# Value products of the attention made in pairs, every fourth slot instead of one every second

## Chip, cores and metric

One core of a Trainium2 chip runs the whole kernel in one launch. The metric is the device time of the launch in microseconds: median 1300.86 of three runs (1298.59, 1300.86, 1301.11).

## What is computed

A decoder layer on x of shape (4, 512, 512), in three residual steps, each on a layer norm of what came before. For the change the middle one matters: attention of 32 query heads over 8 key heads of width 16, in which the context stands in for keys and values.

```python
x = x + mamba_mixer(layernorm(x))
# attention: B = 4 batches, KV = 8 key heads, G = 4 query heads to each, S = 512, D = 16
scores = einsum('bkgsd,bktd->bkgst', qh, kh) / sqrt(D)
weights = softmax(scores, axis=-1)
x = x + einsum('bkgst,bktd->bkgsd', weights, vh)
# feed-forward: a shared expert for all tokens and 2 of 16 routed experts for each token
x = x + shared_expert(layernorm(x)) + routed_experts(layernorm(x))
```

## The kernel before, in words

The kernel has two phases. `stream_phase` (L45 to L1194) does the mixer and the attention of all four batches, and the shared expert and router logits of the first three. `experts_phase` does the same for the last batch, then the routed experts. Between them all engines meet.

**Slots.** The order of the first phase is written out by hand: each engine runs through the same list of slots, `span = range(-LEAD, SLOTS + 8)` (L233), with LEAD = 92 and SLOTS = 4 x 64 = 256, and in each slot issues its pieces of work in a fixed order. Attention is cut into 32 groups (batch and key head), eight slots for each. `n, u = divmod(slot, UNITS)` gives the group and the slot in it. The mixer of batch b runs 92 slots ahead, so that it is over after slot 163; from then on attention is alone but for the shared expert.

**One slot on TensorE** (L1165 to L1194), in this order:

- `scores(slot)` (L1061): two bf16 matmuls of 512 columns, 128 keys against the queries of two heads, into `ps_s`. It waits for the exp of the slot before, for `ps_s` is read by it.
- transposes of queries (L932), of a finished group's output (L939, u = 3) or of its maxima (L946, u = 5), in the slots in which they fall.
- `max_scores(slot + 12)` (L1074): two bf16 matmuls into `ps_m` for the row maxima of a later group, up to slot 243. It waits for the maximum before.
- `front(a, r)` (L1105): from slot 160 on, work of the shared expert of batch a. r counts the slots from 164 + 38a. In r = 0 to 3 tokens are transposed (L1115), in r = 4 the router logits are made (L1124), then 24 matmuls of 512 columns in f32 are spread by `heavy(a, r)` (L210): for batches 0 and 1 one in three slots out of four, for batch 2 one per slot, then two. L1144 makes the gate and up products, L1157 the down product.
- `products(p)` (L1091): the value products of key tile p, four f32 matmuls of 512 columns (listed as eight), one for each query head, each in its own 32 columns of the array (`tile_position=(0, r * VW)`), summed over four key tiles in `ps_o`. It is issued in slot 2p + 3 for p = 0 to 127. It waits for the exps of slots 2p and 2p + 1.

**The other engines.** ScalarE turns `ps_s` into `prob` (L797), a ring of six slots, and waits for the product that frees a place in it (L795 and L796); it copies `ps_o` to `oT` in slot u = 2 (L840), after the fourth product of the group, which is issued in slot u = 1. VectorE takes the maximum of `ps_m` (L654), divides the output by its sum (L697, L700), and for the shared expert takes statistics and normalises (L662, L676) and does the elementwise parts (L682, L687, L692). GpSimd splits maxima and adds the output to the residual; SyncE's queue carries the loads, and the rows of maxima to `q_stack` (L296).

With `heavy`, the slot without a shared expert matmul is slot % 4 = 3 for batch 0 (slots 170 to 201) and slot % 4 = 1 for batch 1 (slots 208 to 239); products fall on all odd slots.

Of the kernel before, what the change touches and what calls it, by code (L numbers as in the profile page):

```python
# [44 lines left out]
def stream_phase(nc, dram, x1, score, ident, identb):  # L45
# [34 lines left out]
    KHALF_AT = (-32, 1)  # L80
    FRONT = SLOTS - LEAD
    WINDOW = 38
    F = 256
    E = 16
    WUP = KD * 2 * F

    with ExitStack() as ctx:
# [117 lines left out]
        def fronting(slot):  # L205

            at = slot - FRONT
            return [(a, at - WINDOW * a) for a in range(B - 1) if -4 <= at - WINDOW * a < WINDOW]

# [9 lines left out]
        def mixing(slot):  # L219

            return divmod(slot + LEAD, PERIOD)

        def batch_at(slot, at):

            b, off = divmod(slot - at, PERIOD)
            return b if off == 0 and 0 <= b < B else None
# [685 lines left out]
        def _(pe):  # L912
# [8 lines left out]
            def transpose_keys(b):  # L921
                pe.wait_ge(s_ctx, 16 * (b + 1))
                claim(s_prest, 5 * b + 1)
                for t in range(TB):
                    ins = nc.tensor.transpose(ps_t[:, t * P:(t + 1) * P], keys[:, t, :], ident[:, :])
                ins.then_inc(s_ptr, 1)

            def transpose_queries(b, c):
                pe.wait_ge(s_q, TB * (b + 1))
                claim(s_prest, 5 * b + c + 2)  # L930
                for t in range(TB):
                    ins = nc.tensor.transpose(ps_t[:, t * P:(t + 1) * P], q[:, t, c * P:(c + 1) * P], ident[:, :])  # L932
                ins.then_inc(s_ptr, 1)

            def transpose_out(n):
                pe.wait_ge(s_otc, n + 1)
                claim(s_fin, n + 1)
                for t in range(TB):
                    ins = nc.tensor.transpose(ps_t[:, t * P:(t + 1) * P], oT[:, t * P:(t + 1) * P], ident[:, :])  # L939
                ins.then_inc(s_back, 1)  # L940

            def transpose_max(n):
                pe.wait_ge(s_msplit, n + 1)
                claim(s_mev, n + 1)
                for t in range(TB):
                    ins = nc.tensor.transpose(ps_tb[:, t * P:(t + 1) * P], mpart[:, t, :], identb[:, :])  # L946
                ins.then_inc(s_mtr, 1)

            def head_means(b):
                pe.wait_ge(s_xs, KI * (b + 1))  # L950
                if b == 0:
                    pe.wait_ge(s_rest, 16 * 10)
                claim(s_gain, b + 1)
                for i in range(KI):
                    for j in range(4):
                        ins = nc.tensor.matmul(ps_t[32 * j:32 * j + 32, 0:P], head_mean[:, i, :],
                                               xz[:, i, j * P:(j + 1) * P], start=(i == 0), stop=(i == KI - 1),
                                               tile_position=(0, 32 * j))
                ins.then_inc(s_mean, 1)

            def outputs(b):
                pe.wait_ge(s_hc, NS * (b + 1))
                claim(s_yrest, b + 1)
                for k in range(NS):
                    ins = nc.tensor.matmul(ps_t[:, :], state_sum[:, k, :], csb[:, k, :],
                                           start=(k == 0), stop=(k == NS - 1))
                ins.then_inc(s_y, 1)

            def transpose_tokens(b, j):
                pe.wait_ge(s_ln, TB * b + j + 1)  # L970
                if b:
                    claim(s_xnT, TB * b + j + 1)
                turned = four[j] if b == 0 else ps_t[:, :]
                for k in range(KD):
                    ins = nc.tensor.transpose(turned[:, k * P:(k + 1) * P], xt[:, j, k * P:(k + 1) * P], ident[:, :])
                ins.then_inc(s_tr, 1)
# [72 lines left out]
            def mixer_half(b, m, h):  # L1049
                at = 2 * m + h  # L1050
                if at == 0:
                    project_steps(b)
                elif 4 <= at < 4 * GROUPS:
                    project(b, m // 2, at % 4)
                elif H2I_AT <= at < H2I_AT + KI:
                    heads_to_inner(b, at - H2I_AT)
                elif OUT_AT <= at < OUT_AT + TB * KI:
                    j, i = divmod(at - OUT_AT, KI)
                    project_out(b, j, i)

            def scores(slot):  # L1061
                n, u = divmod(slot, UNITS)
                g, t = n % G, u // 2
                if u == 0:
                    pe.wait_ge(s_mrow, 48 * (n + 1))
                if slot:
                    pe.wait_ge(s_exp, slot)
                for i in range(2):
                    r = u % 2 * 2 + i
                    ins = nc.tensor.matmul(ps_s[:, i, :], k_stack[:, g, t * P:(t + 1) * P],  # L1070
                                           q_stack[:, g * R + r, :], start=True, stop=True)
                ins.then_inc(s_sc, 1)
# [18 lines left out]
            def products(p):  # L1091
                n, t = divmod(p, TB)
                g = n % G
                pe.wait_ge(s_exp, 2 * p + 2)
                if t == 0:
                    if n:
                        pe.wait_ge(s_otc, n)
                    pe.wait_ge(s_val, n + 1)
                for r in range(R):
                    ins = nc.tensor.matmul(ps_o[r * VW:(r + 1) * VW, :], values[:, t, g, :],  # L1100
                                           prob[:, (2 * p + r // 2) % PROB, r % 2, :],
                                           start=(t == 0), stop=(t == TB - 1), tile_position=(0, r * VW))
                ins.then_inc(s_pv, 1)

            def front(a, r):  # L1105
# [25 lines left out]
                for i in heavy(a, r):  # L1131
                    if i < 16:
# [8 lines left out]
                        if i == 12:  # L1141
                            pe.wait_ge(s_fh, 2 * a + 1)
                        col = k * 2 * F + part * F + f * P
                        ins = nc.tensor.matmul(acc[part], w_shared[:, col:col + P], xnT[:, k, :],  # L1144
# [20 lines left out]
            for slot in span:  # L1165
                b, m = mixing(slot)
                n, u = divmod(slot, UNITS)
                if 0 <= slot < SLOTS:
                    scores(slot)
                if (a := batch_at(slot, K_AT)) is not None:  # L1170
                    transpose_keys(a)
                for c in range(4):
                    if (a := batch_at(slot, C_AT[c])) is not None:
                        transpose_queries(a, c)
                if u == 3 and 0 <= n - 1 < N:
                    transpose_out(n - 1)
                if u == 5 and 0 <= n + 1 < N:
                    transpose_max(n + 1)
                if b < B and m == 32:
                    head_means(b)  # L1180
                if b < B and m == 40:
                    outputs(b)
                if b + 1 < B and m in TURN_AT:
                    transpose_tokens(b + 1, TURN_AT.index(m))
                if b < B:
                    mixer_half(b, m, 0)
                if 0 <= slot + AHEAD < SLOTS:
                    max_scores(slot + AHEAD)
                if b < B:
                    mixer_half(b, m, 1)  # L1190
                for a, r in fronting(slot):
                    front(a, r)
                if slot >= 3 and slot % 2 == 1 and (slot - 3) // 2 < 2 * R * G * TB // 2:
                    products((slot - 3) // 2)  # L1194


def experts_phase(nc, dram, x1, score, ident, out):
# [9 lines left out]
    TOP = 2  # L1207
    F = 256
    KF = F // P
    TILES = (TOP * TOKENS - E) // P + E  # L1210
# [3 lines left out]
    B = 4  # L1214
    WUP = KD * 2 * F
    WCOLS = WUP + KF * D
# [7 lines left out]
    with ExitStack() as ctx:  # L1224
# [66 lines left out]
        xgT = sb("xgT", [P, 2, KD * P])  # L1291
        sg = sb("sg", [P, 2, F])
        sS = sb("sS", [P, KF, 512])
# [544 lines left out]
```

## Time and profile before

| | |
|---|---|
| median of 3 runs | 1300.86 us (1298.59 to 1301.11) |
| profiled execution, its own time | 1302.54 us |
| its span | 1300.7 us |
| TensorE matmul busy | 1224.2 us, 94% |
| VectorE busy | 684.4 us, 53% |
| ScalarE busy | 481.4 us, 37% |
| GpSimd busy | 313.6 us, 24% |
| maximum L654 | 256 times, 1224 ns each |
| exp L797 | 256 times, 1024 ns each |
| value products L1100 | 1024 listed matmuls, 605 ns each |
| mean granted TensorE clock | 0.987 |

Times are of one profiled execution. Matmuls overlap in the array, so that the duration of one listed matmul is longer than its share of the queue: the start of the next one tells that share. An idle time in brackets stands ahead of an instruction, with what ended it. "xN" is the number of listed instructions merged into a row; an f32 matmul is listed as two.

### The profile page before, as it was taken

To read this page: it belongs to the slowest core of one execution; us is meant where nothing else is said; L and a number is where in the kernel's file an instruction comes from. 1 tells how busy PE (TensorE), PEld (TensorE's weight loads), DVE (VectorE), ACT (ScalarE), POOL (GpSimd) and SP (SyncE) were. 2 spreads that over 40 slices of the span, in tenths; PEclk is the share of its full clock that TensorE was granted. 3 is DMA by queue.
4 is the path that set the end of the run, shared out by engine and by line. 5 is a ranking of instruction groups with operands and counts; after the bars stand their busy time and mean duration, and the time that the engine had idled before them with its cause. 6 is when DMAs were issued, how large, how long until landed. Compare 5 with 4: busy or idle time off the path is not lost. (4 is left out here: it accounts for less than half of the span.)

```text
span 1300.7 us, 14817 instructions
## 1 busy us (share of the span) xinstructions
PE 1224.2 (94%) x5045; PEld 508.3 (39%) x5046; DVE 684.4 (53%) x1110; ACT 481.4 (37%) x681; POOL 313.6 (24%) x459
## 2 busy tenths in 40 slices
PE   4989989999999999999999999999978999999996
PEld 2444433333333434333333333333334444444442
DVE  5843585655687465667564766767347222212211
ACT  1311223533554443555353455555510122222221
POOL 3312310221320220221022121111102244333443
PEclk9999999999999999999999999999987999999998
DMA  6320775103274201263400245000029465577641
GB/s 175 100 87 21 184 153 106 31 13 110 68 146 77 66 22 25 82 129 80 100 12 13 94 82 78 34 2 2 33 74 338 103 142 123 154 219 214 177 82 23
DMA packets 113218, 122.71 MB, mean 94 GB/s; under 512 B 19024, under 2 KB 78544, under 8 KB 112896
## 3 DMA queue, kind: packets, MB, share of 16 engines
q1 hardware_dynamic: 102624, 100.76, 29.8%
q0 software_dynamic: 10528, 21.12, 7.9%
q8 instruction: 36, 0.59, 0.2%
q14 instruction: 30, 0.25, 0.1%
HBM read 96.20 MB, written 28.97 MB: 96 GB/s over the span
## 5 line engine op out<-in xcount | busy, mean ns | idle before, releaser
L654 DVE TENSOR_REDUCE mx<-ps_m 128x2 f32<-128x1024 f32 x256 | 313.3, 1224 | 263.1 <-PE ps_m L1087 261.6
L797 ACT ACTIVATE prob<-ps_s 128x1024 f32<-128x1024 f32 x256 | 262.2, 1024 | 380.0 <-PE ps_s L1070 380.0
L1012 PE MATMUL acc<-xnT,wring 128*128 128x512 f32 x560 | 279.7, 599 | 3.5 <-DVE xz L574 1.8
L1708 PE MATMUL ps_gu<-ring,xgT 128*128 x376 | 176.9, 593 | 1.5 <-issue 1.5
L1087 PE MATMUL ps_m<-k_stack,q_stack 96*128 96x512 bf16 x512 | 153.0, 380 | 9.0 <-DVE mx L654 7.3
L1070 PE MATMUL ps_s<-q_stack,k_stack 99*128 99x512 bf16 x512 | 153.8, 382 | 4.4 <-ACT prob L797 4.1
L1442 DVE COPY xgT<-ps_x 128x512 f32<-128x512 f32 x47 | 32.5, 692 | 207.7 <-PE ps_x L1680 203.2
L1100 PE MATMUL ps_o<-prob,values 128*32 128x512 f32 x1024 | 136.4, 605 | 0.0
L1012 PEld LDWEIGHTS acc<-xnT,wring 128*128 128x128 f32 x560 | 102.6, 190 | 69.7 <-issue 34.6
L1402 POOL DMA_INDIRECT out<-y,dest x47 | 74.5, 1585 | 158.8 <-DMA out<-y,dest 115.4
L1070 PEld LDWEIGHTS ps_s<-q_stack,k_stack 99*128 99x128 bf16 x512 | 35.5, 97 | 182.4 <-issue 133.3
L1708 PEld LDWEIGHTS ps_gu<-ring,xgT 128*128 128x128 f32 x376 | 67.6, 190 | 69.8 <-issue 69.8
L1087 PEld LDWEIGHTS ps_m<-k_stack,q_stack 96*128 96x128 bf16 x512 | 45.9, 98 | 123.3 <-issue 76.5
L1724 PE MATMUL ps_yy<-ring,hT 128*128 x188 | 88.5, 593 | 0.9 <-ACT hT L1590 0.9
L1042 PE MATMUL acc<-wring,xz 128*128 128x512 f32 x168 | 85.2, 596 | 0.0
L574 DVE SCALAR_TENSOR_TENSOR xz<-acc,convw,xz 128x511 f32<-128x511 f32 (+2 forms) x84 | 62.7, 746 | 4.2 <-ACT xz L875 2.3
L1597 ACT ACTIVATE y<-ps_yy,share 128x512 f32<-128x512 f32 x47 | 32.3, 687 | 86.3 <-PE ps_yy L1724 77.4
L411 POOL TENSOR_SCALAR mneg<-mx 128x16 f32<-128x16 f32 x32 | 10.0, 313 | 190.2 <-DVE mx L654 190.2
L1389 POOL DMA_INDIRECT xg<-xn_rows,token x47 | 46.7, 993 | 23.4 <-issue 12.5
L1100 PEld LDWEIGHTS ps_o<-prob,values 128*32 128x32 f32 x1024 | 20.1, 108 | 82.1 <-issue 65.4
L1585 ACT ACTIVATE sg<-ps_gu 128x256 f32<-128x256 f32 x47 | 18.0, 384 | 83.1 <-PE ps_gu L1708 81.8
L1144 PE MATMUL acc<-xnT,wring 128*128 128x512 f32 x96 | 48.6, 594 | 0.0
(255 smaller groups left out, 1215.6 us busy)
## 6 DMA issues: line engine op xcount, KB each, us to landing
ring<-in_w_experts SPq DMA_DIRECT2D x96, 256.0 KB
wring<-in_w_in SPq DMA_DIRECT2D x80, 256.0 KB, 3.5
q_stack<-part_rows SPq DMA_DIRECT2D x96, 128.0 KB, 4.8
wring<-in_w_out SPq DMA_DIRECT2D x32, 256.0 KB, 2.7
part_rows<-part SPq DMA_DIRECT2D x20, 384.0 KB, 3.9
xt<-in_x SPq DMA_DIRECT2D x16, 256.0 KB, 4.3
k_stack<-part_rows SPq DMA_DIRECT2D x48, 64.0 KB, 4.0
xn_rows<-xt SPq DMA_DIRECT2D x3, 1024.0 KB, 4.2
```

Of the source, the lines that this page charges most:

```text
L574: ins = nc.vector.scalar_tensor_tensor(out=xz[:, i, tap:], in0=bank(b, 5 + i)[:, :SEQ - tap], scalar=convw[:, i, 3 - tap:4 - tap], in1=xz[ ...
L654: nc.vector.tensor_reduce(mx[:, n % G, 2 * u:2 * u + 2], ps_m[:, :, :], AX.X, ALU.max).then_inc(s_max, 1)
L797: nc.scalar.activation(prob[:, slot % PROB, :, :], ps_s[:, :, :], ACT.Exp, scale=SCALE).then_inc(s_exp, 1)
L1012: ins = nc.tensor.matmul(bank(b, n), weights, xnT[:, k, :], start=(k == 0), stop=(k == KD - 1))
L1042: ins = nc.tensor.matmul(bank(b, OUT_BANK + j), gated[i][:, j * P:(j + 1) * P], ring[:, w % RING, :], start=(i == 0), stop=(i == KI - 1))
L1070: ins = nc.tensor.matmul(ps_s[:, i, :], k_stack[:, g, t * P:(t + 1) * P], q_stack[:, g * R + r, :], start=True, stop=True)
L1087: ins = nc.tensor.matmul(ps_m[:, i, :], q_stack[0:KQ, g * R + r, t * P:(t + 1) * P], k_stack[0:KQ, g, :], start=True, stop=True)
L1100: ins = nc.tensor.matmul(ps_o[r * VW:(r + 1) * VW, :], values[:, t, g, :], prob[:, (2 * p + r // 2) % PROB, r % 2, :], start=(t == 0), sto ...
L1144: ins = nc.tensor.matmul(acc[part], w_shared[:, col:col + P], xnT[:, k, :], start=(k == 0), stop=(k == KD - 1))
L1402: pool.indirect_dma_start(out=out[:, :], out_offset=bass.IndirectOffsetOnAxis(ap=dest[:, n:n + 1], axis=0), in_=y[:, n % YB, :], in_offset ...
L1708: ins = nc.tensor.matmul(ps_gu[p][:, :], xgT[:, p, k * P:(k + 1) * P], weights(own)[:, k * 2 * F:(k + 1) * 2 * F], start=(k == 0), stop=(k ...
L1724: ins = nc.tensor.matmul(ps_y[p][:, :], hT[:, p, k * P:(k + 1) * P], weights(own)[:, WUP + k * D:WUP + (k + 1) * D], start=(k == 0), stop= ...
```

## The change

From slot ALONE = FRONT + 3 = 167 on, TensorE skips `products` in the slots in which p is even, and makes that product directly before the next, odd one. Up to slot 166 nothing differs. Products 82 to 127 are made in 23 pairs, in slots 169, 173 and so on to 257.

```diff
     WINDOW = 38
+    ALONE = FRONT + 3
     F = 256
...
                 for a, r in fronting(slot):
                     front(a, r)
                 if slot >= 3 and slot % 2 == 1 and (slot - 3) // 2 < 2 * R * G * TB // 2:
-                    products((slot - 3) // 2)
+                    p = (slot - 3) // 2
+                    if slot < ALONE:
+                        products(p)
+                    elif p % 2:
+                        products(p - 1)
+                        products(p)
```

## Rows read from the trace of the kernel before

**Rows 1.** Busy time by stretch: slots 170-201, 210-237, and behind the first phase

```profile
core 0: us, PE busy (x) PEld busy (x) DVE busy (x) ACT busy (x) POOL busy (x), PEclk, DMA share, GB/s
753.67:827.81 74.14, 72.22 (x353) 24.38 (x349) 51.85 (x63) 39.14 (x45) 15.37 (x37) 1.00 0.42 70
844.98:907.72 62.74, 62.59 (x303) 20.17 (x299) 41.31 (x46) 33.57 (x38) 7.20 (x24) 1.00 0.01 2
...
962.85:1020.00 57.15, 45.04 (x163) 23.33 (x164) 39.90 (x162) 6.48 (x12) 11.20 (x14) 0.79 0.78 265
```

**Rows 2.** Timeline, TensorE matmuls, slots 190 to 193: start us, duration us, line, shapes

```profile
799.33 0.60 PE L1070 MATMUL ps_s<-q_stack,k_stack 99*128 99x512 bf16 x2
799.77 0.60 PE L1087 MATMUL ps_m<-k_stack,q_stack 96*128 96x512 bf16 x2
800.20 1.02 PE L1144 MATMUL acc<-xnT,wring 128*128 128x512 f32 x2
801.06 0.59 PE L1070 MATMUL ps_s<-q_stack,k_stack 99*128 99x512 bf16 x2
801.68 0.61 PE L1087 MATMUL ps_m<-k_stack,q_stack 96*128 96x512 bf16 x2
802.22 1.06 PE L1100 MATMUL ps_o<-prob,values 128*32 128x512 f32 x8
803.22 0.61 PE L1070 MATMUL ps_s<-q_stack,k_stack 99*128 99x512 bf16 x2
803.66 0.60 PE L1087 MATMUL ps_m<-k_stack,q_stack 96*128 96x512 bf16 x2
...
804.96 0.59 PE L1070 MATMUL ps_s<-q_stack,k_stack 99*128 99x512 bf16 x2
805.58 0.60 PE L1087 MATMUL ps_m<-k_stack,q_stack 96*128 96x512 bf16 x2
806.02 1.02 PE L1157 MATMUL acc<-wring,th 128*128 128x512 f32 x2
806.97 1.06 PE L1100 MATMUL ps_o<-prob,values 128*32 128x512 f32 x8
807.97 0.39 PE L1070 MATMUL ps_s<-q_stack,k_stack 99*128 99x512 bf16 x1
```

**Rows 3.** Timeline of ScalarE and VectorE, slot 192

```profile
803.86 1.02 ACT L797 ACTIVATE prob<-ps_s 128x1024 f32<-128x1024 f32 x1 [1.14 <-PE ps_s L1070]
...
804.29 1.23 DVE L654 TENSOR_REDUCE mx<-ps_m 128x2 f32<-128x1024 f32 x1 [0.74 <-PE ps_m L1087]
```

**Rows 4.** Timeline, TensorE, scores of slots 248 and 249, without max pairs

```profile
931.21 0.60 PE L1070 MATMUL ps_s<-q_stack,k_stack 99*128 99x512 bf16 x2
...
932.93 0.60 PE L1070 MATMUL ps_s<-q_stack,k_stack 99*128 99x512 bf16 x2 [0.26 <-ACT prob L797]
```

**Rows 5.** Timeline, TensorE, matmuls in four 32-column tiles, and the next

```profile
634.58 1.95 PE L956 MATMUL ps_t<-xz,head_mean 128*32 128x128 f32 x64 [0.24 <-DVE ao L700]
636.46 1.12 PE L1012 MATMUL acc<-xnT,wring 128*128 128x512 f32 x2
...
837.99 1.08 PE L1124 MATMUL acc<-xnT,gate_w 128*32 128x128 f32 x32
839.00 0.39 PE L1070 MATMUL ps_s<-q_stack,k_stack 99*128 99x512 bf16 x1
```

**Rows 6.** Timeline, TensorE, scores that begin slots 186, 206, 210, 214 and 218

```profile
790.12 0.61 PE L1070 MATMUL ps_s<-q_stack,k_stack 99*128 99x512 bf16 x2
...
837.02 0.60 PE L1070 MATMUL ps_s<-q_stack,k_stack 99*128 99x512 bf16 x2
...
844.98 0.60 PE L1070 MATMUL ps_s<-q_stack,k_stack 99*128 99x512 bf16 x2
...
854.18 0.60 PE L1070 MATMUL ps_s<-q_stack,k_stack 99*128 99x512 bf16 x2
...
862.82 0.39 PE L1070 MATMUL ps_s<-q_stack,k_stack 99*128 99x512 bf16 x1
```

**Rows 7.** Timeline, TensorE, max pair of slot 238

```profile
908.87 0.39 PE L1087 MATMUL ps_m<-k_stack,q_stack 96*128 96x512 bf16 x1 [0.55 <-DVE mx L654]
```

## Prediction

> **What bounds the kernel now.** The change touches TensorE's order only from slot 167 on, where the mixer is over and attention runs beside the shared expert. I read the busy time by stretch first [rows 1]: TensorE is listed busy for 72.22 of 74.14 us in slots 170 to 201 (the first batch's shared expert) and for 62.59 of 62.74 in slots 210 to 237 (the second's), at a granted clock of 1.00, VectorE for 70 and 66%. That looks like a TensorE bound, and there every switch saved would be time saved. The page warns that ends of matmuls are modelled, so I went on to the matmuls one by one [rows 2]. They show four slots in a row, from the start of one slot's scores to the next: 1.73, 2.16, 1.74 and 3.01 us, 8.64 in sum. From start to start, the score pair takes 0.44 us of the queue, the max pair 0.44, a shared expert matmul ("F") 0.86, a product 1.00 after an entry of 0.09 to 0.10 (F to product 0.95 instead of 0.86, max to product 0.54 instead of 0.44). In the second and fourth slot the max pair starts 0.62 after the scores instead of 0.44: TensorE waited there. So there are two loops beside the queue [rows 2, 3]:
> - scores to exp 0.64, exp 1.02, exp to the next scores 0.08: at least 1.74 us per slot (ScalarE's loop). Where the max pairs are over, 0.44 + 0.86 = 1.30 us of matmuls fill a product-free slot and the next scores still start after 1.72, with 0.26 idle behind the exp [rows 4].
> - max pair to its maximum 0.63, maximum 1.23, to the next max pair 0.06: at least 1.92 us (VectorE's loop).
>
> A product-free slot has 0.44 + 0.44 + 0.86 = 1.74 of matmuls. The pair of a slot without and a slot with product is what hides both loops: while the product runs, the maximum and the exp catch up. That is the cover the change takes away.
>
> **The change, step by step.** It moves 23 products (82, 84 to 126) two slots later, each beside the next one, in slots 169, 173 to 257. Nothing is added: no instruction, DMA or semaphore. No wait gets later in effect: product p waits for exps that the scores before it in the queue have waited for already; the probability buffer of slot s + 1 needs the first product of the burst of slot s, and its exp stands behind scores that come after that burst anyway; the fourth product of a group stays in its slot, so the copy of the output, its transpose and POOL's add keep theirs. SP and POOL are passed by nothing.
>
> *The burst itself.* The trace has no product right behind another. Bounds: at most as alone, 0.09 + 1.00 = 1.09 us; at least 0.86, what F shows for the same 512 columns in f32 [rows 2]. The nearest rows are matmuls in the same four 32-column tiles back to back [rows 5]: 16 of 128 columns take 1.01 to the next instruction, 32 take 1.88, so 16 more cost 0.87, or 0.87 for four tiles of 512 columns. I take 0.86: entry and exit (0.23) are paid once per burst. A pair then costs 0.09 + 0.86 + 1.00 = 1.95. The Trainium skill, "TensorEngine Tiling (Array Packing)", Key Properties, says that changing the tiling mode drains the array; by that rule alone each burst saves one drain and the change is a gain, which is the first rival below. The trace agrees that a switch costs something: the 0.09 ahead of a product and the 0.14 behind it, beyond 0.86, show it.
>
> *First batch's shared expert, slots 170 to 201.* Its matmul-free slot is every fourth, slot % 4 = 3, and the bursts fall on slot % 4 = 1, which has an F. So four slots become F; nothing; F; F + two products. From the end of a burst, t = 0:
> - Slot 2: scores 0, max 0.44, F 0.88; next scores 1.74. Its maximum runs 1.07 to 2.30.
> - Slot 3: max pair at 2.36, queue empty at 2.80. Exp 2.38 to 3.40, next scores 3.48: the queue idles 0.68. Maximum 2.99 to 4.22.
> - Slot 0: max pair only at 4.28, F at 4.72, next scores 5.58. Maximum 4.91 to 6.14.
> - Slot 1: max pair 6.20, F 6.64 to 7.50, two products to 9.45.
>
> 9.45 against 8.64 is +0.81. With the transposes of outputs (0.52 in slot 3) and maxima (0.40 in slot 1) four slots take 9.21 now [rows 2, 6]; by the same steps they become 1.74 + 1.74 + 2.44 + 4.09 = 10.01, +0.80: what the transpose adds in slot 3 is absorbed, but it delays the maximum and comes back in slot 0. Eight such groups of four: **+6.4**.
>
> *Second batch's, slots 210 to 237.* The slots without F are now the burst slots, so work is spread evenly: F 1.74; F 1.92 (max loop); F 1.92; burst 0.62 + 0.44 + 1.95 = 3.01: 8.59, against 8.64 now; with transposes 9.15 against 9.20 [rows 6]. Seven groups: **-0.4**.
>
> *Between.* Slots 206 to 209 (router logits, one F) take 7.96 now [rows 6]; three slots then go by the loops, 1.96 + 1.74 + 1.92, and the burst takes 3.01: **+0.7**. Slots 202 to 205, by the same steps: +0.1. In 238 to 241 the third batch's statistics already hold the max pairs up [rows 7]; one product leaves the waiting and one comes back two slots later: 0. Slots 242 to 245: -0.2. Slots 246 to 253 (F each, no max pairs): 3 x 1.72 + 0.44 + 0.86 + 1.95 = 8.41 against 8.22, twice, less carry: +0.2. The end, slots 254 to 263, is a full queue in which the saved switch counts: -0.3.
>
> Sum: 6.4 - 0.4 + 0.7 + 0.1 - 0.2 + 0.2 - 0.3 = **+6.5 us**. The profiled execution took 1302.54 (span 1300.7 and 1.8 around it), 1.7 over the median 1300.86; against its own time the sum gives 1309.0, against the median **1307.4**. The expert phase behind comes as a block, later by the same amount. What could make it a little more: in slots 174 and 185 and the like a tanh or a multiplication of F stands between the exps or maxima, uncovered now (a few tenths).
>
> **Rivals.**
> 1. *Faster: the queue is the bound.* If TensorE worked through these slots without waiting, as the 62.59 of 62.74 us in [rows 1] suggest, 23 bursts save 0.23 each: -5.3, 1295.6. It decides if the product-free slots last as long as their matmuls; a slot with neither F nor product would then last 0.88. Against it: the max pair 0.62 instead of 0.44 behind the scores [rows 2], and 1.72 us for 1.30 us of matmuls [rows 4]. The point of no change is a second product costing 0.57 (6.5/23 = 0.28 less than I take), below the 0.86 of its columns. 6%.
> 2. *Nothing is saved in the burst.* The second product costs 1.09 because it waits for the first in the same bank. Then 23 x 0.23 = 5.3 more: +11.8, 1312.7. For it: no row shows it at 512 columns. Against: [rows 5]. 13%.
> 3. *No measurable change.* The loops lose 6.5, but slots go faster than my chain has it, or the clock, granted at 0.79 on the mean over the 57 us behind the hand-over to the expert phase [rows 1], comes back a few us earlier. 1301. 8%.
> 4. *It doesn't do what it says*: the condition takes every odd product from 83 to 127 with its forerunner, no product is lost or made twice, so nothing here; under 1%, inside 3.
>
> **How the numbers follow.** The forecast, slower by 4 to 9, has 73%. The range starts at 1303.6 (+2.7: half of the first batch's loss gone) and ends at 1312.6 (rival 2); outside are rivals 1 and 3 and what overshoots 2. A measurement of this kernel tells about 0.2% (2.6 us) from no change. Faster by more 6%; within 8%; slower 86%.
>
> **What would show it.** Slots 170 to 201 about 6.4 us longer (74.1 to 80.5), slots 210 to 237 shorter by 0.4 (62.7 to 62.3); three out of four slots at 1.74 to 2.44; a new idle time of TensorE of 0.6 to 0.7 us behind the exp in slots % 4 = 3 up to 199; the second product 0.86 behind the first; exp and maximum unchanged in number and duration. Wrong would be: the second product at 1.09 (rival 2); first stretch unchanged (rival 1: my loops are not loops); a loss that is spread evenly over both batches, which would mean that the place of the free slot doesn't matter.

## The result, and the profile after

The changed kernel takes 1307.09 us (median of 7 runs, 1303.43 to 1314.69), the kernel before 1300.34 (7 runs, 1296.87 to 1301.11). The ratio is 1.0055, with a 95% interval of 1.0031 to 1.008: slower by 0.3 to 0.8%. Forecast were 1307.4 and slower. Three executions took far longer than the others of their kernel (2495.8 us of the kernel before, 1597.72 us with bursts from slot 205 alone, 4680.28 us of the kernel before with the free slot moved), and the ratios leave them out.

The profiled execution of the changed kernel is the longest of the seven (1314.69 us, span 1312.9). Read as a whole, it would put the loss at 12 us. It has to be read by stretch. Slot 164, three slots ahead of the first difference, begins at 740.46 instead of 738.51 us: 2.0 us of scatter in code that is the same. From there to the first instruction of the expert phase the changed kernel takes 233.67 us instead of 225.88, which is **+7.8**. The expert phase, the same code again, takes 338.8 instead of 336.3.

Busy time by stretch, of the kernel after, for the two stretches of [rows 1] (slots 170 to 201, slots 210 to 237):

```profile
core 0: us, PE busy (x) PEld busy (x) DVE busy (x) ACT busy (x) POOL busy (x), PEclk, DMA share, GB/s
755.69:836.95 81.26, 74.23 (x353) 26.08 (x349) 52.81 (x64) 39.11 (x45) 14.49 (x36) 0.98 0.37 64
854.98:917.72 62.74, 62.07 (x302) 21.72 (x299) 41.73 (x45) 33.43 (x38) 7.18 (x24) 1.00 0.01 2
```

Nearly all of the loss is in the first batch's stretch: 74.14 became 81.26 us, +7.1. The second batch's, with seven bursts in it, took 62.74 before and takes 62.74 now. The matmuls listed are as many as before (353, 302 against 303); TensorE now has 7 us there without any, 5 more than before.

The timeline of TensorE's matmuls for slots 190 to 193, which answers to [rows 2]:

```profile
805.46 0.61 PE L1071 MATMUL ps_s<-q_stack,k_stack 99*128 99x512 bf16 x2
805.90 0.60 PE L1088 MATMUL ps_m<-k_stack,q_stack 96*128 96x512 bf16 x2
806.33 1.02 PE L1145 MATMUL acc<-xnT,wring 128*128 128x512 f32 x2
807.19 0.60 PE L1071 MATMUL ps_s<-q_stack,k_stack 99*128 99x512 bf16 x2
807.82 0.61 PE L1088 MATMUL ps_m<-k_stack,q_stack 96*128 96x512 bf16 x2
808.99 0.59 PE L1071 MATMUL ps_s<-q_stack,k_stack 99*128 99x512 bf16 x2 [0.57 <-ACT prob L798]
809.74 0.60 PE L1088 MATMUL ps_m<-k_stack,q_stack 96*128 96x512 bf16 x2 [0.15 <-DVE mx L655]
810.18 1.02 PE L1158 MATMUL acc<-wring,th 128*128 128x512 f32 x2
811.04 0.59 PE L1071 MATMUL ps_s<-q_stack,k_stack 99*128 99x512 bf16 x2
811.66 0.60 PE L1088 MATMUL ps_m<-k_stack,q_stack 96*128 96x512 bf16 x2
812.11 1.02 PE L1158 MATMUL acc<-wring,th 128*128 128x512 f32 x2
813.06 1.92 PE L1101 MATMUL ps_o<-prob,values 128*32 128x512 f32 x16
814.92 0.39 PE L1071 MATMUL ps_s<-q_stack,k_stack 99*128 99x512 bf16 x1
```

The four slots last 1.73, 1.80, 2.05 and 3.88, together 9.46 us (805.46 to 814.92), where they took 8.64. Read the second slot first: its matmuls need 0.88 us of the queue, and it lasts 1.80, of which 0.57 are put down to the exp. Then the max pair of the third slot comes 0.75 behind its scores instead of 0.44, for the maximum. The burst is the row of 16 listed matmuls: 1.86 us from its start to the next scores, after an entry of 0.09. One product alone has 1.00 in [rows 2]; so the second adds 0.86.

### The profile page after: what moved, and what is told of

The parts are those of the page before. It is cut to its first block and busy times, and to the rows that moved or that the text cites. A ratio compares the mean times of both kernels' runs of the same rounds, so it can differ in the third digit from the quotient of the medians.

```text
span 1312.9 us, 14813 instructions
## 1 busy us (share of the span) xinstructions
PE 1222.5 (93%) x5041; PEld 512.7 (39%) x5046; DVE 684.4 (52%) x1110; ACT 480.7 (37%) x681; POOL 313.0 (24%) x459
## 5 line engine op out<-in xcount | busy, mean ns | idle before, releaser
L1101 PE MATMUL ps_o<-prob,values 128*32 128x512 f32 x1024 | 131.6, 602 | 0.0
```

## The experiments

All kernels are judged by the length of the two stretches (slots 170 to 201 and 210 to 237) in their profile, where a slot repeats within a few hundredths, and by the time only where that can tell. Each ratio is to runs of the kernel before that were made beside it.

**Is it where the free slot stands?** The changed kernel, with the free slot of batch 0 moved onto the burst slots:

```diff
             if a < 2:
-                return () if s % 4 == 1 else (3 * (s // 4) + (s % 4 + 1) // 2,)
+                return () if s % 4 == (3, 1)[a] else (3 * (s // 4) + (s % 4 if a == 0 else (s % 4 + 1) // 2),)
```

> The changed kernel, with batch 0's free slot (no shared expert matmul) moved from slot % 4 = 3 to slot % 4 = 1, onto its burst slots, as batch 1 has it. Theory (the burst costs what it leaves uncovered, and only where a slot with neither matmul nor product arises): slots 170 to 201 fall from 81.3 us to about 74 (the kernel before: 74.1), four plain slots there to 8.6, and the time lands within 0.1% of the kernel before, about 1301. Rival (two products in a row delay scores and maxima, wherever they stand): slots 170 to 201 stay near 81, and the time at 1307.

Measured: 1299.41 us (12 runs), ratio 0.9987 (0.9963 to 1.0012). The stretches, in the order of above:

```profile
754.32:828.49 74.17, 71.53 (x352) 26.09 (x349) 51.36 (x62) 39.01 (x45) 14.51 (x36) 1.00 0.39 70
846.52:909.27 62.75, 62.08 (x303) 21.73 (x299) 41.72 (x45) 33.44 (x38) 7.17 (x24) 1.00 0.01 2
```

All 23 bursts are still there, and 7.1 us are gone by moving eight empty places two slots on. Of these, 0.48 are a fall of the granted clock in the profiled execution of the changed kernel, told of in the last section; 6.6 are the place (80.79 us for the same bursts at full clock, below). A burst as such costs nothing that can be seen in these stretches.

The opposite edit, `(1, 3)[a]` with the forms of the two batches exchanged, takes batch 1's free slot off its bursts:

> The changed kernel, with batch 1's free slot moved from slot % 4 = 1 to slot % 4 = 3, away from its burst slots, as batch 0 has it. Theory: slots 210 to 237 grow from 62.7 us by 7 x 0.8 = 5.6 to 68.4, the whole by about 6 over the changed kernel, 12.7 over the kernel before: 1313. Rival (the loss belongs to batch 0, through the query transposes or the statistics in its slots): slots 210 to 237 stay at 62.7, the time at 1307.

Measured: 1313.62 us (8 runs), ratio 1.0095 (1.0061 to 1.013).

```profile
751.97:833.15 81.18, 74.15 (x353) 26.09 (x349) 52.79 (x64) 39.12 (x45) 14.50 (x36) 0.98 0.37 64
852.04:920.80 68.76, 63.23 (x302) 21.22 (x298) 42.58 (x47) 33.43 (x38) 7.18 (x24) 1.00 0.01 2
```

The second stretch grew by 6.0, the first kept its loss. So the loss doesn't belong to batch 0 (query transposes, statistics); the same pattern costs about the same in the other batch, 0.86 us per group of four against 0.83.

**Which bursts cost?** Bursts up to slot 202 alone, and from 205 alone:

```diff
-                    if slot < ALONE:
+                    if slot < ALONE or slot > 202:
```

> The changed kernel with bursts in slots 169 to 201 alone, single products from 203 on. Theory: the whole loss is here, +6.6 to +7.3 over the kernel before, 1307. Rival (each burst costs about the same 0.3 us): 9 of 23 bursts, +2.6, 1303.

```diff
-    ALONE = FRONT + 3
+    ALONE = FRONT + 39
```

> The changed kernel with single products up to slot 202 and bursts in slots 205 to 257 alone. Theory: +0.7, 1301; slots 210 to 237 unchanged at 62.7. Rival (each burst costs the same 0.3 us): 14 of 23 bursts, +4.1, 1304.5.

Measured: 1305.79 us (10 runs), ratio 1.0039 (1.0015 to 1.0063), for the first; 1301.22 us (12 runs), ratio 0.9993 (0.9965 to 1.0022), for the second. First the two stretches of the one, then of the other:

```profile
751.16:831.95 80.79, 72.72 (x352) 25.52 (x348) 52.46 (x64) 39.12 (x45) 14.50 (x36) 1.00 0.37 65
849.12:911.86 62.74, 62.59 (x303) 20.17 (x299) 41.29 (x46) 33.55 (x38) 7.16 (x24) 1.00 0.01 2
```

```profile
757.70:831.82 74.12, 72.21 (x352) 24.37 (x349) 51.82 (x63) 39.15 (x45) 15.36 (x37) 1.00 0.40 70
849.85:912.59 62.74, 62.07 (x302) 21.74 (x299) 41.73 (x45) 33.46 (x38) 7.20 (x24) 1.00 0.01 2
```

The nine bursts of the first (the one in slot 169 and eight in the stretch) carry +6.65 in slots 170 to 201. Its time alone (0.15 to 0.63% longer) would leave the rival's 1303 open; the stretch doesn't. The fourteen of the second carry +0.9 up to slot 253, of which 0.7 are in slots 206 to 209, and with the end +0.6 from slot 164 to the hand-over. A price per burst is excluded.

**Is the place of the free slot worth something by itself?** The kernel before with the same edit of `heavy` as in the first experiment:

> The kernel before with batch 0's free slot moved from slot % 4 = 3 to slot % 4 = 1, without bursts. Theory: with one product in every odd slot it doesn't matter which of the odd slots has the shared expert matmul; slots 170 to 201 stay at 74.1 us and the time at that of the kernel before. Rival (the new place of the free slot is itself worth some 7 us and would have hidden the burst's loss in the aligned kernel): slots 170 to 201 at 67, the time at 1294.

Measured: 1297.95 us (10 runs), ratio 0.9985 (0.9964 to 1.0007); first stretch:

```profile
756.73:829.98 73.25, 72.11 (x353) 24.43 (x349) 50.92 (x63) 39.01 (x45) 15.31 (x37) 1.00 0.42 71
```

The first seven groups of four slots last as long as before, within 0.04 us. The 0.9 us less come from the eighth, slots 198 to 201 (9.75 instead of 10.60), in which VectorE also takes the statistics of batch 1, and half of that returns in slots 202 to 205 (9.67 instead of 9.21). So the rival's 7 us aren't there, and the place alone is worth 0.4. Against this control, the fair one for the aligned kernel, the bursts aren't quite free: the aligned kernel takes 1.1 us more from slot 164 to the expert phase, with +0.9 in slots 198 to 201, +0.7 in 206 to 209 and -0.3 each in 202 to 205 and at the end, but less than 0.1 in the first seven groups together.

**Two loops, or one?** The maxima over half the keys, in the kernel before and in the changed one. The other half of the maximum is left out; the subtracted value is a little lower for some rows, the rest is computed as before.

```diff
-                nc.vector.tensor_reduce(mx[:, n % G, 2 * u:2 * u + 2], ps_m[:, :, :], AX.X, ALU.max).then_inc(s_max, 1)
+                nc.vector.tensor_reduce(mx[:, n % G, 2 * u:2 * u + 2], ps_m[:, :, 0:SEQ // 2], AX.X, ALU.max).then_inc(s_max, 1)
```

> The kernel before with the row maxima taken over the first 256 of 512 keys (that part of the maximum is left out; the sums are otherwise the same). The maximum should take about 0.7 us instead of 1.23 and VectorE's loop 1.4 instead of 1.92, under ScalarE's 1.74. Expected: four plain slots of batch 0 from 8.64 to 8.28, slots 170 to 201 to 72.5, slots 210 to 237 to 61.6. It is the reference for the next run.

> The changed kernel with the maxima over half the keys. Theory (two loops share the loss): with VectorE's loop short, ScalarE's alone is left: four plain slots of batch 0 are 1.74 + 1.74 + 1.74 + 3.69 = 8.91, slots 170 to 201 about 75.6, that is +3.1 over the kernel before with half maxima where the changed kernel lost 7.1; slots 210 to 237 turn into a gain of 1.5 (60.1). Rival (VectorE's loop is all of it): 170 to 201 no longer than in the other. Rival (neither loop, the products' own length): the loss stays at 7.

Measured in one run each: 1279.28 and 1282.14 us; a maximum took 0.69 us. Stretches of the first kernel, then of the second:

```profile
738.61:810.74 72.13, 71.46 (x353) 24.96 (x349) 35.27 (x62) 39.15 (x45) 14.91 (x37) 1.00 0.43 72
827.71:889.27 61.56, 61.56 (x303) 20.95 (x299) 27.32 (x45) 33.57 (x38) 7.20 (x24) 1.00 0.01 2
```

```profile
737.16:812.71 75.55, 71.54 (x353) 25.73 (x349) 36.13 (x64) 39.11 (x45) 14.38 (x35) 1.00 0.39 69
830.07:890.14 60.07, 60.07 (x303) 21.96 (x299) 28.08 (x47) 33.45 (x38) 7.16 (x24) 1.00 0.01 2
```

With VectorE's loop short, the bursts cost 3.4 us in the first stretch instead of 6.65, and win 1.5 in the second instead of nothing. Both loops are in it, with about half each. VectorE's half is shown by the edit; no run has a shorter exp, so ScalarE's is what remains, read from the trace. What is left of ScalarE's is seen in the timeline of the second kernel, slots 191 and 192:

```profile
785.82 0.60 PE L1071 MATMUL ps_s<-q_stack,k_stack 99*128 99x512 bf16 x2
786.26 0.60 PE L1088 MATMUL ps_m<-k_stack,q_stack 96*128 96x512 bf16 x2
787.62 0.59 PE L1071 MATMUL ps_s<-q_stack,k_stack 99*128 99x512 bf16 x2 [0.77 <-ACT prob L798]
788.05 0.59 PE L1088 MATMUL ps_m<-k_stack,q_stack 96*128 96x512 bf16 x2
```

The free slot still lasts 1.80 us for 0.88 of matmuls, all for the exp; the max pair behind it is no longer late (0.43 after the scores).

**What does a pair save?** The front's work of a burst slot put between the two products:

```diff
+                apart = slot >= ALONE and slot % 4 == 1 and (slot - 3) // 2 < 2 * R * G * TB // 2
+                if apart:
+                    products((slot - 3) // 2 - 1)
                 for a, r in fronting(slot):
                     front(a, r)
...
                     elif p % 2:
-                        products(p - 1)
                         products(p)
```

> The changed kernel with the shared expert's work of a burst slot put between the two products instead of ahead of both, so that each product is entered and left on its own. Theory (a pair saves one switch of 0.23 us): +0.23 in each of the some 15 burst slots that hold such work, slots 170 to 201 from 81.3 to 83.1, the time +3.4 over the changed kernel. Rival (nothing is saved in a burst): no change.

Measured: 1312.85 us (4 runs), ratio 1.0112 (1.0078 to 1.0146). Timeline of the burst in slot 193:

```profile
809.83 0.60 PE L1088 MATMUL ps_m<-k_stack,q_stack 96*128 96x512 bf16 x2
810.37 1.07 PE L1101 MATMUL ps_o<-prob,values 128*32 128x512 f32 x8
811.36 1.12 PE L1158 MATMUL acc<-wring,th 128*128 128x512 f32 x2
812.42 1.07 PE L1101 MATMUL ps_o<-prob,values 128*32 128x512 f32 x8
813.42 0.60 PE L1071 MATMUL ps_s<-q_stack,k_stack 99*128 99x512 bf16 x2
```

The slot lasts 4.21 instead of 3.88. A matmul between two products takes 1.06 of the queue, not the 0.95 it takes ahead of one, so a pair saves 0.33 against this order. The stretch of slots 170 to 201 took 83.46, which is 2.67 more than in the kernel with the same bursts above (80.79), or 8 x 0.33. Nothing saved is excluded; the saving is real and more than paid for.

**Can a wait be used in another way?** The kernel before, single products, with the shared expert's matmul ahead of the max pair in odd slots, and the same for the aligned kernel's burst slots:

```diff
+                fronted = slot > FRONT + 5 and slot % 2 == 1 and slot + AHEAD < SLOTS
+                if fronted:
+                    for a, r in fronting(slot):
+                        front(a, r)
                 if 0 <= slot + AHEAD < SLOTS:
                     max_scores(slot + AHEAD)
                 if b < B:
                     mixer_half(b, m, 1)
-                for a, r in fronting(slot):
-                    front(a, r)
+                if not fronted:
+                    for a, r in fronting(slot):
+                        front(a, r)
```

> The kernel before, single products, with the shared expert's matmul put ahead of the max pair in odd slots from 170 on, so that it fills the 0.18 us for which the max pair waits for VectorE. Theory: slots with matmul and product without transpose go from 3.01 to 2.83; slots 170 to 201 from 74.1 to 72.9, 210 to 237 from 62.7 to 62.2, the whole about -1.8 us, 0.14%, at the edge of what can be told. Rival (the later maximum is waited for in the next slot and the 0.18 comes back there): stretches unchanged.

> The aligned kernel (bursts, with batch 0's free slot on them) with the shared expert's matmul ahead of the max pair in burst slots. There is a matmul in a burst slot only outside the two main stretches, so slots 170 to 201 and 210 to 237 stay at 74.2 and 62.7, and the whole within 0.1% of the aligned kernel. Rival: any gain over the kernel before that front_first doesn't show.

Measured: 1300.35 us (12 runs), ratio 1.0004 (0.9985 to 1.0024), and 1301.3 us (10 runs), ratio 1.0018 (0.9994 to 1.0041). Timeline of slot 193 in the first, and its two stretches:

```profile
802.83 0.60 PE L1070 MATMUL ps_s<-q_stack,k_stack 99*128 99x512 bf16 x2
803.26 1.02 PE L1157 MATMUL acc<-wring,th 128*128 128x512 f32 x2
804.12 0.60 PE L1087 MATMUL ps_m<-k_stack,q_stack 96*128 96x512 bf16 x2
804.65 1.07 PE L1100 MATMUL ps_o<-prob,values 128*32 128x512 f32 x8
805.64 0.39 PE L1070 MATMUL ps_s<-q_stack,k_stack 99*128 99x512 bf16 x1
```

```profile
751.47:824.71 73.24, 72.24 (x352) 24.18 (x349) 50.86 (x62) 39.02 (x45) 15.32 (x37) 1.00 0.40 71
842.14:904.36 62.22, 62.14 (x302) 19.84 (x299) 41.20 (x46) 33.44 (x38) 7.17 (x24) 1.00 0.01 2
```

The slot takes 2.81 instead of 3.01 and the stretches are 0.9 and 0.5 shorter, 1.6 us from slot 164 to the hand-over (224.28 against 225.88). Only the second stretch is shorter for the reason given (three groups without transposes at 8.45 instead of 8.64). In the first, two such groups win 0.2 us each and four with transposes lose 0.09 each, so that the rival is right for part of the slots; nearly all of the 0.9 is in slots 198 to 201 (9.74 instead of 10.60), beside the statistics of batch 1, as in the control. The time doesn't show it: 0.12% is less than the runs can tell. Of the versions that compute everything its trace is the shortest, and whether it is faster than the kernel before stays open. The second is 0.5 us shorter than the aligned kernel from slot 164 to the hand-over (slots 238 to 241 take 10.43 instead of 10.87), and its time shows nothing of it.

## Why the prediction was right, and where its terms were off

Its mechanism holds step by step. The nearness of 1307.4 to the measured 1307.09 is in part luck: by the trace its sum is 1.3 us too low.

- *The bound.* TensorE was not the bound it looks like in [rows 1]; two loops of 1.74 and 1.92 us per slot were, each hidden by the product of the slot. Half maxima took about half of the loss away, the rest stayed with the exp. The Trainium skill, "Perfetto Trace Analysis", Identifying the Most-Contended Engine, says that matmul busy time is no good measure of how close a kernel is to the roofline, because pipelined matmuls look smaller in the trace. The trace agrees that it is no good measure, but here it says too much and not too little: 62.59 of 62.74 us are listed busy, and a shorter maximum still takes 1.2 us off that stretch.
- *Rival 1*, the queue as the bound, needed a free slot as long as its matmuls, 0.88 us where no transpose falls in it; the free slots 191 and 199 last 1.80. *Rival 2*, nothing saved in a burst, needed a second product at 1.09; it takes 0.86. *Rival 3*: two of the seven runs do lie near 1303.5, but the interval doesn't reach 1. *Rival 4* didn't occur: 1024 listed value matmuls before and after.
- *Four slots of batch 0*: forecast 9.45, measured 9.46. Forecast for the ones with transposes 10.01, measured 10.02 (slots 186 to 189: 1.74, 1.71, 2.47, 4.10).
- *Spread unevenly*, as it was written that a loss spread over both batches would refute it: +7.1 and 0.0.
- *Signs that came out otherwise.* The second stretch was to be 0.4 us shorter and is not. The new idle time behind the exp was to be 0.6 to 0.7 us in all the free slots; it is 0.57 where no transpose falls in the slot and 0.15 behind the transposes of an output. The forecast also gives its width twice, as slower by 4 to 9 us and as 1303.6 to 1312.6 (+2.7 to +11.7); the measured lies in both.

Sizes, in slots of the profiled executions:

| slots | forecast | measured |
|---|---|---|
| 164 to 169 | 0 | +0.07 |
| 170 to 201 | +6.4 | +7.12 |
| 202 to 205 | +0.1 | +0.16 |
| 206 to 209 | +0.7 | +0.70 |
| 210 to 237 | -0.4 | 0.00 |
| 238 to 241 | 0 | 0.00 |
| 242 to 245 | -0.2 | +0.05 |
| 246 to 253 | +0.2 | +0.02 |
| 254 to the hand-over | -0.3 | -0.32 |
| sum | +6.5 | +7.8 |

Three terms were too low. In slots 170 to 201, 0.48 of the 0.7 are a fall of the granted clock, below; without it the stretch takes +6.65. The rest there (0.25) and the 0.4 missing in slots 210 to 237 are a few hundredths to 0.17 us in single groups, of two kinds. One is what the prediction named but left out of the sum, an elementwise step of the shared expert between two maxima: slot 225 lasts 3.18 against 3.01 in slot 217, and VectorE's step L683 of the changed kernel stands just ahead of the late maximum. The other it had not seen: slots 212 and 228 last 2.00, where slots 216 and 220 last 1.93. No step of the shared expert stands between their maxima; the max pair starts 0.15 us behind the end of the maximum instead of 0.06, as it does in slots 180 and 196 too. In just these four slots a new pair of key heads begins, for whose queries TensorE waits once more ahead of the max pair (L1078 of the kernel before). Both causes are read from the places, not tried. The third term is slots 242 to 245, 0.25 too low, for which no cause was looked for; the one for slots 246 to 253 was 0.2 too high.

That the median moved by 6.75 and the trace by 7.8 is no conflict: 0.31 to 0.8% are 4.0 to 10.4 us. Nor does 1307.09 confirm the sum to a few tenths. Outside the slots in question the profiled executions differ by more: slot 164 began between 735.94 and 742.53 us, and the expert phase took between 332.1 and 340.2, in the ten profiled executions of kernels with the same code there (all but the two with half maxima).

## What to carry to other kernels

A product or any other filler in a slot is not just work: it is the time in which a single-buffered partner on another engine catches up. Before grouping such fillers to save a switch, write down for every slot the queue's own work and the longest loop through the other engines; where a slot is left with less work than its loop, the loop's length is paid and the group is paid on top. Where filler must be grouped, put the empty places of the other work on the group: here the same 23 bursts cost 7 us or nothing that the time can tell, by a shift of the empty places by two slots.

## What the runs showed of the hardware that was not expected

**The granted clock fell inside the busy phase.** Busy time of the changed kernel in slot 200 and 201, cut at the max pair of slot 200, at the next scores and where the clock is back:

```profile
828.55:830.28 1.73, 0.59 (x2) 0.10 (x3) 1.73 (x3) 1.02 (x1) 0.00 (x0) 1.00 0.00 0
830.28:832.63 2.35, 2.35 (x4) 0.93 (x5) 2.28 (x8) 0.00 (x0) 0.52 (x1) 0.55 0.00 0
832.63:833.50 0.87, 0.87 (x4) 0.27 (x3) 0.84 (x2) 0.00 (x0) 0.52 (x1) 0.50 0.00 0
833.50:836.95 3.45, 3.45 (x22) 0.95 (x20) 3.30 (x6) 1.02 (x1) 0.00 (x0) 0.94 0.00 0
```

The last columns are granted clock, DMA share and GB/s. The clock is granted at 0.50 of 2.4 GHz, its lower level of 1.2 GHz, until about 833.5. Ahead of it TensorE had a free slot (199) and then, from the end of the scores pair to 830.28, no matmul for 1.14 us, for VectorE was at the statistics. In the execution with the same bursts up to 202 the same two slots ran at full clock:

```profile
824.03:827.07 3.04, 1.90 (x7) 0.69 (x8) 3.01 (x6) 1.02 (x1) 0.00 (x0) 1.00 0.00 0
827.07:831.95 4.88, 3.84 (x23) 1.01 (x21) 4.82 (x12) 1.02 (x1) 1.04 (x1) 1.00 0.00 0
```

7.92 us against 8.40: the fall cost 0.48. It appears in this stretch in two of the five executions that have these bursts away from the free slot (mean clock 0.98 there: the changed kernel and the misaligned one), and in none of the others (1.00). The same wait of 1.14 us stands in the execution at full clock (3.04 - 1.90 in its first row), so it isn't enough by itself. A loss of cover may thus cost clock too, but three of the five executions don't show it; what decides it was not tried.

**A switch costs in both directions, and more around a lone matmul.** A product alone costs 0.09 + 1.00 of the queue, the second of a pair 0.86, and a shared expert matmul of the whole array between two products 1.06 instead of 0.86. The Trainium skill, "TensorEngine Tiling (Array Packing)", Key Properties, says that a change of the tiling mode drains the array. The trace agrees that each change costs time: a pair saves 0.23 us against two single products and 0.33 against the split order.
